# One layer on one core: prologue in another order, low-rank products stacked as float32r pairs, gates turned one step later, and one bias product moved to POOL

## The reference

```python
x = x + layernorm(attention(layernorm(x)))       # q, k with rotary turn, softmax, Wo
n = layernorm(x)
base = n @ W.T
proj = l2norm(n @ Wp.T + bp);  logits = proj @ l2norm(sim) * exp(temp)
lw = softmax(logits);  gate = lw where it is the largest of the 4, else 0
res = sum_e gate[e] * (n @ Wd_e.T) @ Wu_e.T      # ranks 1, 2, 4, 8: 15 columns in all
x = x + layernorm(base + res)
```

## Time and profile before

| what | value |
|---|---|
| time, median of 3 runs | 150.28 us (150.28 to 150.42) |
| the profiled execution | 150.36 us, of which the span from first to last instruction is 148.6 us and 1.76 us lie around it |
| PE busy | 132.5 us (89% of the span) |
| DVE busy | 129.8 us (87%) |
| ACT busy | 112.2 us (76%) |
| POOL busy | 87.3 us (59%) |
| granted TensorE clock, mean | 0.966 |
| time from one pass to the next, passes 2 to 5 | 14.6 us |

### The profile page before, as it was taken

One profiled execution on the slowest core, in us unless ns is written; L12 is line 12 of the kernel. 1 busy time (PEld: TensorE's weight loads), 2 busy tenths in 40 slices (PEclk: granted clock), 3 DMA queues, 4 the chain that ended last, 5 costly groups with the idle time before them and its releaser, 6 DMA issues.

```text
span 148.6 us, 3108 instructions
## 1 busy us (share of the span) xinstructions
PE 132.5 (89%) x883; PEld 107.0 (72%) x883; DVE 129.8 (87%) x574; ACT 112.2 (76%) x376; POOL 87.3 (59%) x148
## 2 busy tenths in 40 slices
PE   0989789999989999999999999999999998985470
PEld 0667567889878879887988798779878986963230
DVE  6878969989897999999999999789789898899933
ACT  3656395987978899789969996999699948664450
POOL 6320806641918595769576856788556964348552
PEclk9999999999999999999999999999999999999655
DMA  2633340000000000200020002000100010000013
GB/s 92 180 113 90 84 128 4 2 0 0 0 7 0 2 0 0 71 4 0 2 75 2 0 0 75 0 0 0 71 7 2 25 46 4 0 0 0 2 71 141
DMA packets 5266, 4.83 MB, mean 32 GB/s; under 512 B 594, under 2 KB 5250, under 8 KB 5250
## 3 DMA queue, kind: packets, MB, share of 16 engines
q1 hardware_dynamic: 5104, 4.51, 9.6%
q10 hardware_dynamic: 146, 0.13, 0.3%
HBM read 2.54 MB, written 2.10 MB: 31 GB/s over the span
## 4 chain that ended last, share of the span: by engine, by line
PE 71%; DVE 15%; ACT 5%; POOL 2%; issue 2%; DMA 2%; POOLq 1%; DVEq 0%; ACTq 0%
PE ps_s L1321 10%; PE ps_a L1341 9%; PE ps_z L1364 5%; PE ps_b L1341 4%; PE ps_a L1331 4%; PE ps_c L1341 4%; PE ps_b L1331 3%; PE ps_s L1352 2%; PE ps_c L1331 2%; PE ps_c L1310 2%; PE ps_z L1377 2%; PE ps_s L1310 2%; PE ps_d L1300 2%; PE ps_d L1298 2%; PE ps_d L1299 2%
## 5 line engine op out<-in xcount | busy, mean ns | idle before, releaser
L432 ACT ACTIVATE probs<-ps_s,neg_max 128x256 f32<-128x256 f32 x60 | 25.3, 488 | 9.7 <-DVE neg_max L669 9.6
L669 DVE TENSOR_REDUCE neg_max<-ps_s 128x2 f32<-128x512 f32 x30 | 20.3, 681 | 1.2 <-PE ps_s L1321 1.1
L1321 PE MATMUL ps_s<-qk_t 64*128 64x256 f32 x120 | 17.4, 409 | 0.0
L1341 PE MATMUL ps_a<-v_all,probs_t 128*128 128x129 f32 x120 | 16.5, 280 | 0.0
L1341 PEld LDWEIGHTS ps_a<-v_all,probs_t 128*128 128x128 f32 x120 | 14.6, 191 | 2.0 <-issue 2.0
L689 DVE SCALAR_TENSOR_TENSOR x_all<-y_all,rsy,x_all 128x128 f32<-128x128 f32 x32 | 14.0, 462 | 1.3 <-POOL rsy L294 0.7
L1321 PEld LDWEIGHTS ps_s<-qk_t 64*128 64x128 f32 x120 | 10.6, 191 | 5.0 <-issue 4.3
L279 POOL TENSOR_TENSOR turn<-qk,sin_x 128x256 f32<-128x256 f32 x15 | 11.0, 733 | 2.5 <-ACT qk L418 2.1
L282 POOL TENSOR_TENSOR qk<-qk,cos_x 128x256 f32<-128x256 f32 x15 | 11.7, 777 | 1.2
L290 POOL TENSOR_TENSOR inv_norm<-norm,power 128x4 f32<-128x4 f32 x7 | 7.2, 1027 | 8.3 <-DVE norm L738 8.3
L306 POOL TENSOR_TENSOR std<-ve,root 128x4 f32<-128x4 f32 x7 | 7.1, 1019 | 8.2 <-DVE ve L710 8.2
(11 more groups left out here) (336 smaller groups left out, 432.0 us busy)
## 6 DMA issues: line engine op xcount, KB each, us to landing
x_all<-x SPq DMA_DIRECT2D x7, 256.0 KB, 2.7
out<-x_all SPq DMA_DIRECT2D x7, 256.0 KB, 2.1
x_all<-x SPq DMA_DIRECT2D x2, 128.0 KB, 2.7
out<-x_all SPq DMA_DIRECT2D x2, 128.0 KB, 1.7
w_raw<-w_attn ACTq DMA_DIRECT2D x1, 128.0 KB, 2.7
w_raw<-w_attn SPq DMA_DIRECT2D x1, 128.0 KB, 3.0
bo_bp<-vectors SPq DMA_DIRECT2D x1, 80.0 KB, 3.3
ffn_raw<-w_ffn SPq DMA_DIRECT2D x1, 71.5 KB
```

The lines of the kernel that those rows point to most:

```text
L432: last = act.activation(probs[:, u, j, :], scores_of(n, u)[:, j * T:(j + 1) * T], ACT.Exp, bias=neg_max[:, u, j:j + 1])
L669: dve.tensor_reduce(neg_max[:, u, :], scores_of(n, u)[:, :].rearrange("p (j k) -> p j k", j=TILES), AX.X, ALU.max, negate=True).then_inc(m ...
L1321: last = pe.matmul(scores_of(n, 2 * b + h)[:, j * T:(j + 1) * T], qk_t[r, b, 0, j * P:(j + 1) * P], qk_t[r, b, 1, :], start=True, stop=True)
L1341: last = pe.matmul(unit_of(n, u)[:, j * VW:(j + 1) * VW], probs_t[:, u, i, j * P:(j + 1) * P], v_all[:, at:at + VW], start=(i == 0), stop= ...
```

## The change

Four things are changed together.

**The low-rank product.** The gates are split into an upper part, rounded to float32r, and a lower part, the rest. `gated` gets 64 columns per row tile: upper, lower, upper again at an offset of 32; `wu_z` holds upper and lower weights in the same 32-row blocks. One product of 128 rows by 256 columns in float32r then gives all the partial products of two row tiles. DVE writes the gates in three instructions (`gate`, the upper parts in one instruction of 120 columns, `gates_low`) where one was; PE transposes twice where it did once; ACT copies 256 columns where it copied 128. In the end part the two halves of pair 7 are treated alike.

**The turn of the gates.** In the passes, `turn_gated` stands behind `weigh(a, 0)` and no longer ahead of it, and `low_rank` behind `weigh(a, 1)` and no longer ahead of it. ACT's order is unchanged.

**The product of deviation and routing bias.** `scaled_bias` leaves DVE and stands on POOL right behind `deviation`, ahead of `rope(a+1, 1)`.

**The prologue.** The first factors of pair 0 are worked out ahead of the rotary frequencies, the statistics of pair 1 are spread over earlier gaps on DVE, the copy of `turned` follows the first q and k copy on ACT, ACT normalises all four row tiles of pair 1 (and of no other pair), and `rows_up(1)` stands ahead of the copies of v of pair 0.

```diff
@@ POOL
+            def scaled_bias(n):
+                pool.wait_ge(std_ready, n + 1)
...
+                pool.tensor_tensor(bias_s[:, :, :], bias_b[:, :].unsqueeze(1).to_broadcast([P, PT, RW]),
+                                   std2[:, :].unsqueeze(2).to_broadcast([P, PT, RW]), ALU.mult).then_inc(scaled, 1)
...
                 if has(a - 1):
                     deviation(a - 1)
+                    scaled_bias(a - 1)
                 if has(a + 1):
                     rope(a + 1, 1)
@@ ACT
             def normalise(n):
-                for t in (2, 3):
+                for t in (2, 3) if n > 1 else range(PT):
...
             def gated_copy(n):
                 act.wait_ge(dt_done, n + 1)
-                act.activation(gated_t[:, :], (ps_b if n >= LAST - 2 else ps_d)[:, 0:P], ACT.Copy).then_inc(dt_out, 1)
+                act.activation(gated_t[:, :, :].rearrange("p k c -> p (k c)"), (ps_b if n >= LAST - 2 else ps_d)[:, 0:2 * P], ACT.Copy).then_inc(dt_out, 1)
...
                 if a == 0:
+                    rows_up(1)
                     v_first(0)
-                    rows_up(1)
                     v_first(1)
@@ DVE
-                dve.tensor_tensor(gated[:, :, 0:RANK], picked[:, :, :], rank_wide(total), ALU.mult).then_inc(gated_ready, 1)
+                dve.tensor_tensor(gate[:, :, :], picked[:, :, :], rank_wide(total), ALU.mult)
+                up = gated[:, :, :].rearrange("p t (s l) -> p t s l", s=2)[:, :, :, 0:RANK]
+                dve.tensor_tensor(up, picked[:, :, :].unsqueeze(2).to_broadcast([P, PT, 2, RANK]),
+                                  total[:, :].unsqueeze(2).unsqueeze(3).to_broadcast([P, PT, 2, RANK]), ALU.mult).then_inc(gate_up, 1)
+
+            def gates_low(n):
+                dve.wait_ge(gate_up, n + 1)
+                dve.tensor_tensor(gated[:, :, RANK:2 * RANK], gate[:, :, :], gated[:, :, 0:RANK].bitcast(F32), ALU.subtract).then_inc(gated_ready, 1)
...
             last.then_inc(shift1, 1)
-            dve.wait_ge(shift1, 1)
-            for t in (0, 1):
-                dve.tensor_scalar(xn[:, t, :], x_all[:, rows(1, t)], rs1[:, 1, t:t + 1], nm1[:, 1, t:t + 1],
-                                  ALU.mult, ALU.add).then_inc(xn_ready, 1)
+            later_weights(0)
...
-                if last_:
-                    scaled_bias(a - 1)
                 if now:
                     add_head(a, 2, 0)
@@ PE
+                if now:
+                    weigh(a, 0)
                 if done:
                     turn_gated(a - 2, (v_out, 4 * (a + 1) + 2) if nxt else (v_out, 4 * PAIRS) if now else (dt_out, a - 2))
                 if now:
-                    weigh(a, 0)
+                    weigh(a, 1)
                 if done:
                     low_rank(a - 2)
-                if now:
-                    weigh(a, 1)
```

More of the change, by code:

```diff
@@ L331, in end_factors_z, with first_factors @@
                 pool.tensor_tensor(rsz_e[:, half(k)], var_e[:, half(k)], power[:, half(k)], ALU.pow).then_inc(rstdz_e, 1)
+            def first_factors(k):
+                pool.wait_ge(var0, k + 1)
+                pool.tensor_tensor(rs1[:, 0, half(k)], ve1[:, 0, half(k)], power[:, half(k)], ALU.pow).then_inc(rstd0, 1)
+            first_factors(0)
             pool.wait_ge(base_ready, 1)
             pool.tensor_tensor(freq_c[:, 3:4], freq_c[:, 2:3], expo[:, :], ALU.pow).then_inc(inv_ready, 1)
-            for k in range(2):
-                pool.wait_ge(var0, k + 1)
-                pool.tensor_tensor(rs1[:, 0, half(k)], ve1[:, 0, half(k)], power[:, half(k)], ALU.pow).then_inc(rstd0, 1)
+            first_factors(1)
             pool.wait_ge(late_loaded, 32)
@@ L368, in _ @@
             deviation(LAST - 1)
+            scaled_bias(LAST - 1)
             scaled_guards(LAST - 1)
@@ L924, in later_weights @@
                     dve.wait_ge(post_mm, 2)
-                    for t in range(PT):
-                        rr = slice(LANE * t, LANE * (t + 1))
-                        last = dve.tensor_copy(wu_z[rr, t, :], ps_z0[rr, 0:E])
+                    link(dve.tensor_copy(wu_spare[:, :], ps_z0[:, 0:E]), post_link)
+                    for t in range(2):
+                        up, low = slice(2 * LANE * t, 2 * LANE * t + LANE), slice(2 * LANE * t + LANE, 2 * LANE * (t + 1))
+                        dve.tensor_copy(wu_z[up, t, :], wu_spare[up, :].bitcast(F32))
+                        last = dve.tensor_tensor(wu_z[low, t, :], ps_z0[low, 0:E], wu_spare[low, :].bitcast(F32), ALU.subtract)
                     last.then_inc(post_dve, 1)
@@ L1022, in _ @@
             dve.tensor_tensor(spatial, spatial, turn[:, 0, :, :, :].rearrange("p g h i -> p g (h i)"), ALU.add).then_inc(rope0_done, 1)
+            stats(1, 2)
             first_low(1)
-            for t in range(PT):
-                stats(1, t)
+            stats(1, 3)
             gap(1)
@@ L1104, in _ @@
                     mean(a + 3)
+                if done:
+                    gates_low(a - 2)
+                if has(a + 3):
                     variance(a + 3)
@@ L1202, in _ @@
             add_head(LAST, 2, 0)
+            gates_low(LAST - 2)
             add_head(LAST, 2, 1)
-            scaled_bias(LAST - 1)
             weights_sum(LAST, 3)
@@ L1370, in turn_gated @@
                 pe.wait_ge(*bank_free)
-                pe.transpose((ps_b if n >= LAST - 2 else ps_d)[:, 0:P], gated[:, :, :].rearrange("p t c -> p (t c)"), ident[:, :]).then_inc(dt_done, 1)
+                for k in range(2):
+                    last = pe.transpose((ps_b if n >= LAST - 2 else ps_d)[:, k * P:(k + 1) * P],
+                                        gated[:, 2 * k:2 * k + 2, :].rearrange("p t c -> p (t c)").bitcast(F32), ident[:, :])
+                last.then_inc(dt_done, 1)
             def low_rank(n):
@@ L1403, in end_turn_gated @@
                     pe.wait_ge(x2t_out_e, 2)
-                pe.transpose(gated_bank[k][0:2 * LANE, 0:P], gated_e[:, half(k), :].rearrange("p t c -> p (t c)"),
+                pe.transpose(gated_bank[k][:, 0:P], gated_e[:, half(k), :].rearrange("p t c -> p (t c)").bitcast(F32),
                              ident[:, :]).then_inc(dt_done_e, 1)
```

73 lines of the change are left out of this document (44 added, 29 removed).

## The result

The changed kernel takes 151.20 us (median of 5 runs, 151.04 to 151.28), against 150.28 before (5 runs): a ratio of 1.0053, with a 95% interval from 1.0038 to 1.0068. It is slower, by 0.9 us, where the forecast was 151.4. The profiled execution took 151.28 us, 0.92 more than that of before.

The account below looks back on a forecast made before the run. PE was taken to set the pace in passes 2 to 6, with little slack, and DVE's short routing instructions the end; -0.65 + 0.64 + 0.79 + 0.38 = +1.16 on 150.36, less 0.08, gave 151.4 us, range 149.1 to 152.6.

Parts of the forecast that it names:

- Stacked product: PE, passes 2 to 6: float32r product 0.24 for 0.63, one more transpose 0.11; 0.28 less per pass without waits.
- Passes 2 to 5: Gates turned later: ACT's lateness makes PE stand still 0.44, each pass 0.16 longer, +0.64 for four passes.
- ACT's part: Passes: ACT idles 0.63 ahead of its copy of the gates, making the last softmax weights 0.75 late.
- the one that ends last: Passes: ACT's stall, not DVE's 0.3 lateness, taken as what finally holds PE, 0.16 per pass.
- slower by more: Rival, passes: POOL's operations catch DVE's new instructions, 0.35 later per pass in 2 to 4; 152.0 to 152.9, chance 0.12.
- Pass 6: Bias product on POOL (0.74) and square root 0.60 later delay PE's turn after `rope(7, 1)`: +0.79, bounds 0.2 to 0.9.
- Prologue: Start of kernel: `turn_x` stays at 18.28, PE's 0.53 wait ahead of 21.55 goes: -0.65, bounds 0 to -1.5.
- A new gap on PE early in the prologue: Ahead of 12 us, a gap would keep PE's clock low for longer and shrink the prologue gain; not priced.
- End: After the passes: last turn of gates 1.2 later, shorter float32r products recover most: +0.38, between 0 and +0.8.

Follow-up runs that it names:

- old PE order: Changed kernel with PE's order as before: gates' turn ahead of the first weighing, product ahead of the second; 150.11 us, ratio 0.9984.

## Why the prediction was right, and where its sum was not

**Stacked product.** Two products of 256 columns take 0.33 (84.08, the next row at 84.41), not 0.24, and the two turns 0.22 as forecast. The saving itself is real: with no wait, pass 5 is 0.35 shorter than before (old PE order), forecast 0.28. It is made up otherwise, since PE also spends 0.90 and 0.81 on the two `weigh` there, where it spent 0.99 and 0.91.

**Passes 2 to 5: +0.64 forecast, +1.03 measured (0.26, 0.26, 0.24 and 0.27).** ACT's part held: 0.52 of idle time for 0.63, 0.71 late for 0.75, and in pass 5 PE turns the last softmax weights 5.01 behind the turn, 0.23 later than the 4.78 of before (4.88 in passes 2 to 4), forecast 0.16. What failed is the step that takes the stall by ACT as "the one that ends last". In passes 2 to 4 it is DVE's last row. PE turns it 4.64 behind the turn, and that turn, half a microsecond long, stands ahead of the fourth turn of softmax weights, which then starts at 5.14, 0.13 later than ACT alone would have it.

The forecast's own figures say so once they are carried through. It had DVE 0.3 later: the last row at 86.73 + 0.3 = 87.03, `turn_x2` at 87.08, and the fourth turn 0.49 behind that (87.27 - 86.78), at 87.57, which is later than ACT's 87.43 and makes 0.30 per pass instead of 0.16. It set DVE's row beside ACT's weights and left out the turn that stands between them on PE. Measured, the turn of the last row came 4.64 behind instead of 4.39, 0.25 later.

These 0.25 are not the case "slower by more", in which POOL's operations catch the new instructions. They do catch `mean` now, but they let go of the pair of rows in return. From the reciprocal of `total` to the start of the fourth row maximum DVE takes 3.19 in pass 4, and 2.93 before. The two new instructions add 0.19 + 0.13 = 0.32, and what POOL holds comes out nearly even, a little less than before. This is read from the rows; no run took the split of the gates out of the passes.

**Pass 6: +0.79 forecast, +0.60 measured.** The chain is the one forecast: the square root starts at 116.96 right behind POOL's scale, which ACT's squares made late, then the bias product, 0.60 and not 0.74 long, then `rope`, the rows with one more between them:

```profile
116.96 1.01 POOL L309 TENSOR_TENSOR std<-ve,root 128x4 f32<-128x4 f32 x1
118.05 0.60 POOL L317 TENSOR_TENSOR bias_s<-bias_b,std 128x248 f32<-128x248 f32 x1
...
120.22 0.72 POOL L288 TENSOR_TENSOR qk<-qk,turn 128x256 f32<-128x256 f32 x1
```

PE comes late to this place by itself, since it had waited for ACT, so that only 0.25 of waiting is left. Undoing the product gives 0.30 here.

**Prologue: -0.65 forecast, -0.66 at pass 1.** The agreement is luck. The new prologue alone is worth 0.93, and something else in the change, by the rows the second copy for the stacked weights, takes 0.27 of it back; the forecast had neither. The two rows on PE came as forecast: 18.28 unmoved, and 20.99, with no wait, for 21.55. A new gap on PE early in the prologue, which the forecast feared for the clock, did come (0.79 ahead of 11.04); whether it cost anything, no run tells.

**Pass 1: nothing forecast, -0.58 measured.** A wait of 0.62 for DVE's last row was there before, the same kind as now in passes 2 to 4. I had read the passes from pass 4 and never looked at pass 1. By the rows it went because POOL's `rope` came 0.18 later against DVE's rows, a side effect and nothing that the change aims at. It is not the bias product: with that back on DVE, pass 1 stays 13.92.

**End: +0.38 forecast, +0.53 measured.** The last turn and the two products answer to the earlier trace rows:

```profile
143.38 0.48 PE L1440 MATMUL ps_c<-ident,gated_e 128*128 128x128 f32 x1 [0.46 <-DVE gated_e L930]
143.50 0.56 PE L1445 MATMUL ps_a<-wu_z,gated_t_e 128*128 128x256 f32 x1
144.22 0.58 PE L1445 MATMUL ps_d<-wu_z,gated_t_e 128*128 128x256 f32 x1 [0.15 <-ACT gated_t_e L503]
```

Against the pass before it, the last turn is 1.44 late (1.82 - 0.38), forecast 1.2, and the short products give most of it back, as forecast. The second of them is done 0.74 behind the first, though, and not 0.4. Of the 0.53, 0.20 is the bias product on POOL, which I had not priced here; that the rest, 0.3, is the gates of pairs 5 and 6 is by subtraction, since in the changed kernel the form of the last pair made no difference. No run took those gates apart.

So -0.66 - 0.58 + 1.03 + 0.60 + 0.53 = +0.92, against -0.65 + 0.64 + 0.79 + 0.38 = +1.16. The gain missed in pass 1 (0.58) and the loss missed in the passes (0.39) nearly cancel, which is why the time came out closer than its terms.

## What to carry to other kernels

Where two engines deliver to the bound engine with little slack each, compute the lateness of both for every pass and take the maximum: a fix of one shows only what the other leaves (0.40 and 0.38 apart, 1.33 together). An engine that does short dependent work beside another's long operations needs its order checked against those operations: moving the short instructions out of the way put the long rows there (2.0 us worse). And a step that is put off for one engine (turn the gates later, for DVE) has to be priced pass by pass: with the early turn passes 2 to 4 were as long as with the late one, and pass 5 was 0.62 shorter. Its neighbours' order has to be chosen with it.

## What the runs showed of the hardware

A DVE instruction on four columns takes 0.69 to 0.73 beside POOL's rotation of 256 columns and 0.20 to 0.24 beside one of 32, which was shown by changing POOL's size alone. The Trainium skill, SBUF — State Buffer, § Who interferes with whom, has the rule: a DVE instruction with two inputs in SBUF contends with a POOL instruction that reads SBUF, and the port pair that they share is an exclusive lock. For POOL's operations of 256 columns the runs agree. Beside POOL's powers of four columns, which read SBUF too, they show no hold. The same `mean` and `ve`, in pass 1 of the changed kernel, stand inside a power of 1.01:

```profile
36.95 1.01 POOL L266 TENSOR_TENSOR rs<-ve,power 128x4 f32<-128x4 f32 x1
37.48 0.17 DVE L665 SCALAR_TENSOR_TENSOR mean<-tmp,stats 128x4 f32<-128x4 f32 x1
37.75 0.16 DVE L670 SCALAR_TENSOR_TENSOR ve<-tmp 128x4 f32<-128x4 f32 x1
```

So a POOL row's length in the timeline does not say how long it holds DVE; why the powers do not, no run tells. The same section says that copies can take part when their operands meet certain conditions, and the copy of 30 columns above, 0.71 for what took 0.19 with 60 columns just ahead of it, agrees. The row maxima, which read PSUM, kept their 0.67 to 0.69 in every pass.

What had not been expected is how much the phase is worth: less than 0.2 us of start time between a pair of rows and POOL's operation decided 0.6 us of one pass, 1.67 or 1.07.
